# Attention with top-1 experts: turning the normalised rows in VectorE blocks through memory in place of TensorE transposes

## What is computed

```python
h = layernorm(x)                                  # x: (32, 256, 256)
q, k, v = (split_heads(h @ W.T + b) for W, b in ((Wq, bq), (Wk, bk), (Wv, bv)))
scores = einsum('bhqd,bhkd->bhqk', q, k) / sqrt(32)
attn = softmax(where(adj == 0, -inf, scores))
x = x + einsum('bhqk,bhkd->bhqd', attn, v).reshape(b, n, 256) @ Wo.T + bo
x = x + moe(layernorm(x), controller, f1, f2)     # 64 experts, top 1 of each 16 rows
```

## Time and profile before

| | |
|---|---|
| median of 3 runs | 770.58 us |
| the profiled execution | 772.04 us |
| its span | 770.2 us |
| attention, batch 0 to the end of batch 31 | about 23 to 515 us |
| TensorE busy | 712.3 us (92%) |
| VectorE busy | 605.7 us (79%) |
| ScalarE busy | 546.5 us (71%) |
| GpSimd busy | 127.6 us (17%) |
| mean granted TensorE clock | 0.987 |

### The profile page before, as it was taken

One profiled execution on the slowest core, in us unless ns is written; L12 is line 12 of the kernel. 1 busy time (PEld: TensorE's weight loads), 2 busy tenths in 40 slices (PEclk: granted clock), 3 DMA queues, 4 the chain that ended last, 5 costly groups with the idle time before them and its releaser, 6 DMA issues.

```text
span 770.2 us, 22457 instructions
## 1 busy us (share of the span) xinstructions
PE 712.3 (92%) x7206; PEld 554.9 (72%) x7206; DVE 605.7 (79%) x2574; ACT 546.5 (71%) x1622; POOL 127.6 (17%) x130
## 2 busy tenths in 40 slices
PE   8899999999999999999999999878999989987936
PEld 7788887888888788878888888656565555554613
DVE  6699999998998999999989998877656656655612
ACT  3799988998898989899988998745454454452500
POOL 2210001000100100010001001636325225200000
PEclk9999999999999999999999999999999999999969
DMA  6776786787677767867877777650599999999999
GB/s 181 188 175 158 175 195 147 172 195 164 164 184 166 188 161 166 195 151 168 191 166 170 158 167 162 160 207 2 233 333 307 388 319 300 389 312 322 392 346 306
DMA packets 121495, 166.01 MB, mean 216 GB/s; under 512 B 15296, under 2 KB 84416, under 8 KB 121184
## 3 DMA queue, kind: packets, MB, share of 16 engines
q1 hardware_dynamic: 118944, 163.18, 75.6%
q10 hardware_dynamic: 2304, 1.58, 0.8%
q0 software_dynamic: 192, 0.52, 0.2%
HBM read 47.78 MB, written 41.94 MB: 116 GB/s over the span
## 4 chain that ended last, share of the span: by engine, by line
PE 47%; DVE 22%; issue 14%; DMA 8%; SPq 3%; ACT 3%; DVEq 2%; POOL 0%; POOLq 0%
PE bank L593 7%; PE bank L769 6%; DMA stage<-scratch 5%; PE bank L748 5%; PE bank L606 4%; PE bank L617 4%; PE bank L567 4%; PE bank L580 4%; DVE Ps L1125 4%; DVE PTs L1136 3%; PE bank L737 3%; PE bank L545 3%; SPq L397 2%; DVE nmax L1125 2%; DVE stats L1066 2%
## 5 line engine op out<-in xcount | busy, mean ns | idle before, releaser
L913 ACT ACTIVATE Ps<-Ps,nmax 128x256 f32<-128x256 f32 x512 | 254.7, 501 | 22.7 <-DVE nmax L1125 21.4
L1125 DVE CUSTOM_DVE_ANT_0 Ps<-bank,masks 128x256 f32<-128x256 f32 x512 | 195.7, 420 | 16.2 <-issue 16.0
L593 PE MATMUL bank<-ident,Ps 128*128 128x128 f32 x1024 | 134.8, 274 | 5.1 <-ACT Ps L913 2.6
L593 PEld LDWEIGHTS bank<-ident,Ps 128*128 128x128 f32 x1024 | 114.2, 140 | 13.9 <-issue 5.3
L545 PE MATMUL bank<-hT,WT 128*128 128x256 f32 x512 | 121.1, 380 | 0.4 <-ACT hT L870 0.4
L463 POOL TENSOR_TENSOR X<-X,bob 128x512 f32 (+1 forms) x32 | 41.1, 1286 | 391.8 <-ACT hn L878 389.0
L545 PEld LDWEIGHTS bank<-hT,WT 128*128 128x128 f32 x512 | 92.4, 190 | 10.8 <-ACT Vs L886 0.8
L475 POOL TENSOR_SCALAR h<-X,mv,roots 128x256 f32<-128x256 f32 x64 | 79.3, 1250 | 113.9 <-PE bank L737 80.4
L913 ACT ACTIVATION_READ_ACCUMULATOR Ps<-Ps,nmax 128x1 f32 x512 | 97.5, 191 | 0.0
L580 PE MATMUL bank<-stack 128*128 128x256 f32 x512 | 91.4, 311 | 0.0
L1136 DVE COPY PTs<-bank 128x512 f32<-128x512 f32 x128 | 87.6, 684 | 0.2
(11 more groups left out here) (92 smaller groups left out, 1000.3 us busy)
## 6 DMA issues: line engine op xcount, KB each, us to landing
stack<-parts SPq DMA_DIRECT2D x506, 128.0 KB, 2.5
scratch<-stage SPq DMA_DIRECT2D x64, 512.0 KB, 4.3
stage<-scratch SPq DMA_DIRECT2D x96, 256.0 KB, 4.5
X<-in_x SPq DMA_DIRECT2D x32, 256.0 KB, 2.9
rbc<-turned SPq DMA_DIRECT2D x128, 64.0 KB, 2.1
out<-X SPq DMA_DIRECT2D x32, 256.0 KB, 4.4
XRlast<-scratch SPq DMA_DIRECT2D x16, 512.0 KB, 8.1
f1s<-in_L_ffn_f SPq DMA_DIRECT2D x1, 2048.0 KB, 9.0
```

The lines of the kernel that those rows point to most:

```text
L593: last = nc.tensor.transpose(PTb[h % 2][:, k * N + t * P:k * N + t * P + P], Ps[:, pr % 2, t, h % 2, k * P:k * P + P], ident[:, :])
L913: last = nc.scalar.activation(Ps[:, pr % 2, t, h, :], Ps[:, pr % 2, t, h, :], ACT.Exp, bias=nmax[:, pr % 2, t, h:h + 1], scale=-1.0, accum ...
L1125: last = nc.vector.tensor_tensor_reduce(out=Ps[:, pr % 2, t, h, :], in0=s_bank(n)[:, h * N:h * N + N], in1=masks[:, t, :], scale=1.0, scal ...
```

## The change

The normalised rows of batches 2 to 31 take another way. `apply_norm` writes `hn` with its columns in another order of blocks; VectorE's new `turn_h` turns it in 32x32 blocks into `T2` (one instruction of 128x512); GpSimd writes `T2` to a DRAM tensor `blocks` with 4 DMAs, waits until they have landed, and reads it back with 2 DMAs into `hT`, which now has two halves by parity and lies in `f2s`. Batches 0 and 1 keep the TensorE transposes. The order of the columns is carried through by the order of the mask's rows and by `normalise`, which becomes two instructions.

The Newton rounds and the shift go to GpSimd (`refine`, 15 dependent instructions on 128x4); VectorE keeps sums, the first step and the guess. The spread of the reciprocals (L1144) goes to GpSimd too. `add_bo` becomes two instructions. `save_pt(b, 4)` goes from VectorE to ScalarE. The orders of all engines change.

```diff
 # GpSimd
+            def write_blocks():
+                for a in range(QUARTERS):
+                    nc.gpsimd.dma_start(blocks.rearrange("(m j) (a f) -> j m a f", m=HPG, a=QUARTERS)[:, :, a, :],
+                                        T2[32 * a:32 * a + 32, :].rearrange("p (m f) -> p m f", m=HPG)).then_inc(h_out, 16)
+            def read_blocks(par):
+                for k in range(KT):
+                    nc.gpsimd.dma_start(hT[:, par, k, :].rearrange("p (a e) -> p a e", a=QUARTERS),
+                                        blocks.rearrange("p (a k e) -> p k a e", a=QUARTERS, k=KT)[:, k, :, :]).then_inc(hT_in, 16)
+            def refine(b):
+                X, Y, A, C = (root[:, j, :] for j in range(4))
...
+                pool.wait_ge(guess_done, b + 1)
+                link(nc.gpsimd.tensor_tensor(X, X, minus_half, ALU.mult))
+                for i in range(3):
+                    link(nc.gpsimd.tensor_tensor(A, Y, Y, ALU.mult))
+                    link(nc.gpsimd.tensor_tensor(C, A, X, ALU.mult))
+                    link(nc.gpsimd.tensor_tensor(C, C, three_halves, ALU.add))
+                    link(nc.gpsimd.tensor_tensor(Y, Y, C, ALU.mult))
+                link(nc.gpsimd.tensor_tensor(A, mv[:, :, 0], Y, ALU.mult))
+                nc.gpsimd.tensor_tensor(shift[:, :], A, minus_one, ALU.mult).then_inc(root_done, 2)
             def batch(b, par, last):
-                add_bo(b, par, last)
+                if in_loop(b) or b > 0:
+                    spread_reciprocals(prev(b))
+                if par == 1 and (in_loop(b) or b + 4 < B):
+                    refine(b)
+                coming = in_loop(b) or b + 2 < B
+                pool.wait_ge(ln_done, b + 1)
+                if coming:
+                    pool.wait_ge(h_turned, b + 1)
+                    pool.wait_ge(v_ready, b + 1)
+                add_bo(b, 0)
+                if coming:
+                    write_blocks()
+                    pool.wait_ge(h_out, (b + 1) * (16 * QUARTERS))
+                add_bo(b, 1)
+                if coming:
+                    read_blocks(par)
 # TensorE
+            def hT_arrived(b):
+                if isinstance(b, int) and b < 2:
+                    return hT_saved, b + 1
+                return hT_in, (b - 1) * (16 * KT)
+            def q_project(b, par):
+                pe.wait_ge(*hT_arrived(b))
             def batch(b, par, last):
-                if not (first or last):
-                    k_project(b + 1)
                 scores(b, par, 0)
                 scores(b, par, 1)
+                if not last:
+                    q_project(b + 1, 1 - par)
                 if not first:
                     p_transpose(prev(b), 6)
+                if not (first or last):
+                    k_project(b + 1, 1 - par)
+                scores(b, par, 2)
+                scores(b, par, 3)
+                if not first:
                     p_transpose(prev(b), 7)
-                if not last:
-                    q_project(b + 1)
+                scores(b, par, 4)
                 if not first:
                     pv(prev(b), 1 - par, 0)
                     pv(prev(b), 1 - par, 1)
-                scores(b, par, 2)
-                scores(b, par, 3)
-                scores(b, par, 4)
                 p_transpose(b, 0)
+                scores(b, par, 5)
                 p_transpose(b, 1)
...
-                if not late:
-                    h_transpose(b + 2)
 # ScalarE
             def batch(b, par, last):
+                if not late:
+                    apply_norm(b + 2, par)
+                exps(b, 0)
                 if not last:
-                    save_k(b + 1, 1 - par)
+                    save_q(b + 1, 1 - par)
+                    if not first:
+                        save_k(b + 1, 1 - par)
...
-                if not late:
-                    save_hT(b + 2)
...
                 save_pt(b, 5)
+                save_pt(b, 4)
 # VectorE
+            def turn_h(b):
+                dve.wait_ge(ln_done, b + 1)
+                if in_loop(b) or b > 2:
+                    dve.wait_ge(hT_in, (b - 2) * (16 * KT))
+                nc.vector.transpose(T2[:, :], hn[:, :, :].rearrange("p t d -> p (t d)")).then_inc(h_turned, 1)
             def batch(b, par, last):
                 maximum(b, 0)
+                maximum(b, 1)
                 if not first:
+                    turn(prev(b))
                     save_pt(prev(b), 6)
+                if not (isinstance(b, int) and b >= B - 2):
+                    turn_h(b + 2)
+                if not last:
+                    for which in ((1, 0) if first else (0, 1)):
+                        save_low(b + 1, 1 - par, which, 0)
+                        save_low(b + 1, 1 - par, which, 1)
+                maximum(b, 2)
+                maximum(b, 3)
                 if ahead:
                     sums_of(b + 3)
+                    dve.wait_ge(root_done, b + 3)
                     mean_variance(mv, 2 * QT)
...
+                norm_step(0)
+                save_pt(b, 0)
+                norm_step(1)
                 maximum(b, 4)
...
-                save_pt(b, 4)
 # SyncE: the mask's rows by quarters
-                    sp.dma_start(adjs, adj.rearrange("(t p) k -> p t k", p=P)).then_inc(adj_in, 16)
+                    for r in range(QUARTERS):
+                        own = adj[(r % 2) * P + (r // 2) * 32:(r % 2) * P + (r // 2) * 32 + 96, :]
+                        sp.dma_start(adjs[32 * r:32 * r + 32, 0, :], own[0:32, :]).then_inc(adj_in, 16)
+                        sp.dma_start(adjs[32 * r:32 * r + 32, 1, :], own[64:96, :]).then_inc(adj_in, 16)
```

More of the change, by code:

```diff
@@ L451, in _ @@
                 nc.gpsimd.memset(tie[:, 0, t:t + 1], float(values[t])).then_inc(zeroed, 1)
+            for j, value in enumerate((-0.5, 1.5, -1.0)):
+                nc.gpsimd.memset(newton[:, j, :], value).then_inc(newton_set, 1)
             pool.wait_ge(q_saved, 1)
@@ L458, in _, with spread_reciprocals @@
             pool.wait_ge(bias_done, 1)
[L460 to L463, removed]
+            pool.wait_ge(newton_set, 3)
+            def spread_reciprocals(b):
+                pool.wait_ge(rsum_done, b + 1)
+                if in_loop(b) or b > 0:
+                    pool.wait_ge(turn_done, b)
+                every = [P, G * QT * HPG, 32 // HPG]
+                nc.gpsimd.tensor_tensor(spread[:, 0, :].rearrange("p (s d) -> p s d", d=32 // HPG),
+                                        rsum[:, :, :, :].rearrange("p g t h -> p (g t h)").unsqueeze(2).broadcast_to(every),
+                                        nans[:, :, :, :].rearrange("p g t h -> p (g t h)").unsqueeze(2).broadcast_to(every),
+                                        ALU.mult).then_inc(spread_done, 1)
@@ L869, in save_hT @@
                 act.wait_ge(hT_ready, b + 1)
-                nc.scalar.copy(hT[:, :, :], src[:, :]).then_inc(hT_saved, 1)
+                for k in range(KT):
+                    last = nc.scalar.copy(hT[:, b, k, :].rearrange("p (a t i) -> p t a i", t=QT, a=QUARTERS),
+                                          src[:, k * N:k * N + N].rearrange("p (t a i) -> p t a i", t=QT, a=QUARTERS))
+                last.then_inc(hT_saved, 1)
             def apply_norm(b, par):
@@ L890, in save_high @@
                 act.wait_ge(ready, b + 1)
-                if which == 1 or isinstance(b, int) and b == 0:
+                if which == 0 or isinstance(b, int) and b < 2:
                     for j in range(HPG):
@@ L969, in batch @@
                     save_one_hot(0, M[0])
+                exps(b, 5)
                 exps(b, 6)
@@ L1093, in first_step, with step @@
                         .then_inc(root_done, 1)
-            def step(i, b):
+            def step(i, b, guess=None):
                 chain_wait()
@@ L1100, in step @@
                         dve.wait_ge(ln_done, b)
-                if i < ROOT_STEPS:
+                if i == 1 and guess is not None:
+                    root_step(i, mv[:, :, 1], root).then_inc(guess_done, 2)
+                elif i < ROOT_STEPS:
                     mark(root_step(i, mv[:, :, 1], root))
@@ L1270, in batch @@
                     tied_logits(0, M[0])
-                save_pt(b, 0)
-                if last:
                     group_maximum()
-                norm_step(0)
-                maximum(b, 5, lambda: norm_step(1))
+                maximum(b, 5, lambda: norm_step(2))
                 if last:
@@ L1299, in _ @@
             chain[0], chain[1] = chain[0] + chain[1], 0
+            turn(B - 1)
             save_pt(B - 1, 6)
```

149 lines of the change are left out of this document (82 added, 67 removed).

## The result

The changed kernel takes 1024.8 us (median of 4 runs, 1020.9 to 1029.1) against 770.0 us for the kernel before beside it (769.4 to 773.2): a ratio of 1.328, 95% interval 1.325 to 1.331. The forecast was 947 us, 850 to 1065.

The account below looks back on a forecast made before the run. TensorE was taken to bound the attention. Waits for `hT` and lost clock add 12.7 us a pair, 14 times, 177 us: 772.0 + 177 - 1 = 948, given as 947 us, range 850 to 1065.

Parts of the forecast that it names:

- What decides: Landing of `hT` for batch b + 2: TensorE waits 11.2 us at the q projection of batches 2, 4, ..., 28.
- Q(odd) to the guess: From an odd batch's q projection on TensorE to VectorE's guess of the roots in that batch: 9.9 us.
- writes, issue to landing: GpSimd's four writes to memory: the last starts after 3 x 0.55 and lands 3.0 later, 4.65 us.
- reads, issue to landing: GpSimd's two reads into `hT`: the second starts after 1.0 and lands 3.8 later, 4.8 us.
- Q(even) to Q(odd): Even batch's q projection to the odd one's: TensorE needs 17.05 us with clock loss, the rows' path 16.5, just hidden.
- a pair: Two successive attention batches, odd and even: 42.95 us for 30.28, so 12.7 more, 14 times.
- the second starts after the first's issue, for which I take 1.0: GpSimd's two reads back: the second read was to start 1.0 us after the first.
- my addition of 0.9 from a crowded stretch: GpSimd's DMA path taken as 0.9 us longer than SyncE's, from 4.4 against 3.5 us; landings 3.0 and 3.8.
- (a): Rival: GpSimd's issue time grows with a DMA's pieces, write 1.65 and read 6.05 us; about 1360 us, chance 0.12.
- (b): Rival: an odd batch's write and read do not wait for the guess, path 14.3 us hidden; 757 us, chance 0.05.
- (c): Rival: TensorE's stall is there but short, with no clock loss; 780 to 850 us, chance 0.08.
- The ideal gain: TensorE's `h_transpose` leaves 30 batches at 0.44 us each, saving 13.2 us if nothing else were later.

Follow-up runs that it names:

- all mended: Changed kernel with refine behind the transfers, 1536 bytes for descriptors and VectorE's turn ahead of head 6's copy: 781.2 us, ratio 1.011 to 1.016.
- the best order tried: Changed kernel without the write to memory and read back, with head 7's transposes ahead of scores 2 and 3: 769.1 us, ratio 0.993 to 0.998.
- two runs: Both on the kernel without the crossing: head 4's copy back on VectorE, 779.6 us; head 7's transposes ahead of scores 2 and 3, 769.1 us.
- the run with 46 matmuls: Changed kernel with 46 extra 128x128 matmuls on TensorE filling its wait ahead of the q projection in even batches: 983.2 us.

## Why the prediction was right, and where it was off

**What decides.** Right: TensorE waits for `hT` at the q projection in the even batches, 9.9 to 10.9 us for the forecast 11.2, since `refine` stands ahead of the writes; the run that swaps the two settles it. Not right was that the odd batches have nothing like it: they wait 2.1 to 4.0 us. The granted clock's mean is 0.893 for the forecast 0.85, and the attention ends near 768 us for 690.

**The sum, term by term.** Measured from 231.20 to 258.45 us: 27.25 us for the forecast 25.9.

| term | forecast | measured |
|---|---|---|
| Q(odd) to the guess | 9.9 | 11.8 (to 242.96) |
| refine | 5.3 | 4.2 |
| writes, issue to landing | 4.65 | 4.2 |
| reads, issue to landing | 4.8 | 5.7 |
| Q(even) to Q(odd) | 17.05 | 19.4 |
| a pair | 42.95 | 47.1 |

The two halves are single ones; the pair is the mean over nine, from GpSimd's first addition of an odd batch, 247.19, to that nine pairs later, 671.28. The step that was mis-sized is "the second starts after the first's issue, for which I take 1.0": it started after 2.9 us in odd batches and 3.7 to 4.8 in even ones. In the odd ones the shorter refine and writes make up for it. In the even one shown the reads took 223.53 to 231.20 = 7.7 us for 4.8, so that the path was 19.4 us for 16.5 and was no longer "just hidden". Behind that a second clock loss followed, which the forecast had in even batches only: the odd batch's projections took 2.51 and about 2.7 us for 1.89, and with them Q(odd) to the guess grew to 11.8. In three odd batches the clock held (the q projection took 1.99 us at 186.41, 326.53 and 609.50), and there it was 10.1 us, close to the forecast 9.9. With 1536 bytes the pair was 206.09 to 247.23 = 41.1 us, 1.8 under the forecast. 4.15 us a pair are 58 of the 78 us between 947 and 1025; the other 20 lie mostly in the batches ahead of and behind the 14 pairs, which I had given only the saving: TensorE waited for rows in batches 1, 29 and 30 as well, 5.66, 3.81 and 4.05 us, each time with the projection behind it at 3.4 to 3.7 us. The time came out in the range with the terms erring both ways: `refine` and the writes were shorter than forecast, the reads, the clock and the ends longer.

**The bounds and durations.** `turn_h` took 0.702 us for my 0.70; a link of `refine` 0.28 for 0.35. The four writes landed 2.3 us after issue for my 3.0, by the median. The estimate of 2.15 from the Trainium skill (DMA: Bandwidth & Descriptors, section "Anatomy of one DMA — SWDGE (gpsimd) path") was the better guide there, and my addition of 0.9 from a crowded stretch the worse; for the reads (median 3.5) it was the other way, 2.3 against my 3.8.

```profile
L500 POOL DMA_DIRECT2D blocks<-T x120: 548/561/608, 27.2 to 711.5; - x120
...
DMA to landing us min/median/max: 1.9/2.3/3.5
```

```profile
L506 POOL DMA_DIRECT2D f2s<-blocks x60: 752/761/786, 32.4 to 718.5; - x60
...
DMA to landing us min/median/max: 2.6/3.5/6.0
```

**The rivals.** (a), that an issue grows with its pieces, is false in size: 0.56 us with 128 pieces and 0.76 with 512. It also took packets for pieces: the profile counts 32 packets for a write and 48 for a read, the 48 of the four DMAs that (a) scaled from, and not 144 and 528. Yet it pointed near the right object, if the number of pieces costs through the room for them. (b), that the path is hidden, did not happen. The run that moves `refine` makes its condition true, and took 888 us and not 757: the path that (b) reckons at 14.3 us was longer, above all by the second read, which GpSimd issued 3.4 us late in the mean of that run too. With all mended the 757 us do not come either. (c) did not happen.

**The ideal gain.** "0.44 x 30 = 13.2 us" fell as a gain: without any crossing it was 0, with the best order tried 3. I had set the engines' work against TensorE's and found it less, and did not look at what TensorE would wait for in the new order: at the products with V 9.9 us in 340, where it had been 1.7. What these waits come from was narrowed by two runs, not found.

## What to carry to other kernels

When work moves to an idle engine, write down that engine's new order with the time at which each wait ends; an instruction that waits for something late belongs behind everything that is ready earlier. Two hops through memory in series need their whole latency, both landings and both issues, to fit between making and use, and the room for descriptors must hold what is in flight at once. A saving on the busiest engine is worth nothing until the waits that the others would then cause have been looked for one by one.

## What the runs showed of the hardware that I had not expected

GpSimd's second DMA of 512 pieces started 2.1 to 4.0 us late (once 5.6) with 1024 bytes for descriptors and at once with 1536; the profile gives this idle time no cause. A DMA issue on GpSimd costs 0.56 us with 128 pieces and 0.76 with 512. A dependent chain of 128x4 operations on GpSimd runs at 0.28 us a link, for VectorE's 0.20. The clock fell behind some waits as short as 1.9 to 3 us, and eight matmuls then took 3.2 to 3.7 us for 1.9; behind others of the same length (2.55 us at 87.06 in the run with 46 matmuls) they took 2.0. In three of the short waits the granted clock stood at 1.00 to their end and fell only when the work had resumed.
